# Handing the middle third of a bilinear sampler's sums to GpSimd, and turning each tile's samples one tile later

## What is computed

```python
x = x + _L0_conv_ref(_gn(x), ...)   # 8x8 patches, top-1 of 8 experts' 3x3 convolutions, ReLU
x = x + _L1_conv_ref(_gn(x), ...)   # 3x3 convolution whose weights are mixed from 4 by a routing
x = x + _L2_conv_ref(_gn(x), ...)   # nearest of 512 codebook vectors for every pixel
x = x + _L3_conv_ref(_gn(x), ...)   # bilinear sampling at 9 offsets per pixel, then a 3x3/stride-3 conv
```

## Time and profile before

| | before |
|---|---|
| median of 3 runs (lowest to highest) | 2382.57 us (2381.78 to 2383.68) |
| the profiled execution | 2377.75 us |
| its span | 2375.9 us |
| mean granted TensorE clock | 0.941 |
| busy PE / PE weight loads / DVE / ACT / POOL | 83% / 72% / 74% / 64% / 5% of the span |
| fronts | the instruction at L538, one in each front, starts from 233.8 to 2137.3 us |

### The profile page before, as it was taken

The page is one execution under the profiler, slowest core; times in us unless marked ns, Lnnn a source line. Parts: engine busy times, 40 slices in busy tenths (PEclk is TensorE's granted clock), DMA queues, the critical chain, the costliest instruction groups (busy, mean ns, idle before and its releaser), DMA issues.

```text
span 2375.9 us, 51549 instructions
## 1 busy us (share of the span) xinstructions
PE 1978.7 (83%) x20746; PEld 1699.7 (72%) x20746; DVE 1767.3 (74%) x3541; ACT 1525.7 (64%) x1787; POOL 111.6 (5%) x90
## 2 busy tenths in 40 slices
PE   0345579899798989989798898989799897989999
PEld 0212567789577976788677896778777895779998
DVE  2167368977698777987689876987679766997776
ACT  0022457677576865768576766767667675769886
POOL 2000000010000000010000100000000100001000
PEclk9877689999899998999899998999899998999999
DMA  6743854465444752556544763447535553223321
GB/s 185 147 118 94 188 143 140 134 170 160 119 138 127 192 163 89 174 120 173 140 144 124 186 168 106 163 112 191 153 113 159 143 147 98 71 74 114 115 108 52
DMA packets 258752, 323.93 MB, mean 136 GB/s; under 512 B 201268, under 2 KB 212244, under 8 KB 254292
## 3 DMA queue, kind: packets, MB, share of 16 engines
q1 hardware_dynamic: 240644, 274.52, 41.5%
q0 software_dynamic: 3280, 29.86, 5.1%
q10 hardware_dynamic: 14592, 16.26, 2.7%
HBM read 251.21 MB, written 55.99 MB: 129 GB/s over the span
## 4 chain that ended last, share of the span: by engine, by line
PE 47%; DVE 24%; DVEq 13%; issue 5%; DMA 4%; ACTq 3%; ACT 2%; SPq 2%; POOL 0%; POOLq 0%
PE bank L1105 33%; DVE samp L803 6%; DVEq L802 5%; DVE code L975 5%; DVEq L974 5%; PE bank L1092 3%; PE bank L1203 3%; PE bank L1162 3%; PE bank L1189 3%; DVE onehot L982 2%; SPq L392 2%; DVE top L973 2%; ACTq L588 1%; DVEq L999 1%; ACTq L638 1%
## 5 line engine op out<-in xcount | busy, mean ns | idle before, releaser
L1105 PEld LDWEIGHTS bank<-picture,tent 128*128 128x128 f32 x9216 | 1328.9, 195 | 145.2 <-issue 133.3
L1105 PE MATMUL bank<-picture,tent 128*128 128x160 f32 x9216 | 1391.1, 307 | 7.8 <-issue 4.5
L586 ACT ACTIVATE tent<-zs,row_at_sb 128x1152 f32<-128x1152 f32 x512 | 640.8, 1252 | 72.4 <-PE bank L1105 28.2
L798 DVE TENSOR_TENSOR strip<-bank,near 128x480 f32<-128x480 f32 x768 | 499.7, 651 | 215.7 <-PE bank L1105 214.2
L590 ACT ACTIVATE tent<-tent 128x2304 f32<-128x2304 f32 x256 | 543.9, 2125 | 18.8 <-issue 0.3
L803 DVE TENSOR_REDUCE samp<-strip 128x96 f32<-128x480 f32 x768 | 501.5, 653 | 70.9 <-issue 0.9
L1092 PE MATMUL bank<-ident_sb,samp 128*96 128x128 f32 x768 | 137.8, 290 | 179.9 <-DVE samp L803 118.7
L1203 PE MATMUL bank<-cb,xs 128*128 128x512 f32 x512 | 274.1, 618 | 14.1 <-ACT xs L654 7.9
L1092 PEld LDWEIGHTS bank<-ident_sb,samp 128*96 128x96 f32 x768 | 82.3, 130 | 206.8 <-DVE samp L803 145.0
L575 ACT COPY samp_t<-bank 96x384 f32<-96x384 f32 x256 | 119.7, 468 | 153.7 <-PE bank L1092 108.3
L654 ACT COPY xs<-xn 32x128 f32<-32x128 f32 x256 | 75.8, 296 | 171.6 <-PE bank L1203 154.8
(11 more groups left out here) (124 smaller groups left out, 1007.1 us busy)
## 6 DMA issues: line engine op xcount, KB each, us to landing
zs<-z_rows SPq DMA_DIRECT2D x256, 576.0 KB, 4.1
picked_weights<-arena SPq DMA_DIRECT2D x15, 1800.0 KB
arena<-picked_weights SPq DMA_DIRECT2D x24, 720.0 KB, 6.6
arena<-windows SPq DMA_DIRECT2D x288, 50.0 KB, 2.7
slice<-picked_weights SPq DMA_DIRECT2D x16, 720.0 KB, 6.7
windows<-arena SPq DMA_DIRECT2D x32, 312.5 KB, 6.1
slice<-windows SPq DMA_DIRECT2D x192, 50.0 KB, 2.3
arena<-xp SPq DMA_DIRECT2D x48, 136.0 KB, 4.9
```

The source lines that it names most:

```text
L586: act.activation(w[:, piece], zs[:, N % SPREADS, :], ACT.Abs, bias=row_at[:, piece:piece + 1])
L798: dve.tensor_tensor(y, STRIPS[J % 3][:, 0:DENSE * XW * C].rearrange("p (d c x) -> p d c x", d=DENSE, c=C), w.broadcast_to([128, DENSE, C, ...
L1105: m = pe.matmul(STRIPS[j % 3][:, XW * C * e:XW * C * (e + 1)], tent[:, N % TENTS, c, DENSE * d + e], picture[:, b % 2, i, c], start=(c == ...
```

## The change

- The middle third of each tile (`d == 1`) is multiplied by DVE but no longer summed by it: GpSimd adds its five columns in three instructions (192, 96 and 96 elements per partition), each waiting for the one before, and signals `middle_ready`. `strip` gets three buffers, one for each `d`; DVE's next middle multiply waits for `middle_ready`, and so does the turn. To make room in SBUF, `SPREADS` goes from 4 to 3.
- The turn of tile N-1 moves from behind the first third of tile N to behind its last third, `copy_samples` from `d == 1` one tile on to `d == 0` two tiles on, `convolve` from `d == 2` of tiles 4, 8, ... to `d == 1` of tiles 5, 9, ..., `copy_result` from `d == 0` to `d == 2` of these.
- `row1` and `row3` give a third each to `pool`, which has 5 now. They are spread over its steps: one between statistics and aggregation of the normalisation, one behind the normalisation, one before and one behind the routing product on DVE, one among the mixing instructions. ACT's exponent comes behind the second third of `pool` instead of behind all.
- GpSimd's own steps move: windows into `y`, the gathers behind `norm2` and behind half of `scores`, the subtraction behind the thirds of `rows`, the clip behind four thirds of `near`. SP's `store_weights(k, 1)` and `load_slice(k, 0)` come later.

```diff
-SPREADS = 4
+SPREADS = 3
-        strip = sb("strip", [128, 2, DENSE * C, XW])
+        strip = sb("strip", [128, THIRDS, DENSE * C, XW])
-        ... ("row0", 8), ("row1", 8), ("row2", 8), ("row3", 8), ("y", 7), ("features", 1), ("pool", 3),
+        ... ("row0", 8), ("row1", 7), ("row2", 8), ("row3", 7), ("y", 7), ("features", 1), ("pool", 5),
...
@@ SP, scores @@
-                    if t == 5 and k:
+                    if t == 6 and k:
                         store_weights(k, 1)
-                    if t == 6 and k:
-                        load_slice(k, 0)
                 at("spell")
                 at("pick")
+                if k:
+                    load_slice(k, 0)
@@ GpSimd @@
+            def third(J):
+                N, d = divmod(J, THIRDS)
+                if d != 1:
+                    return
+                y = strip[:, 1]
+                pool.wait_ge(strip_read, J + 1)
+                pool.tensor_tensor(y[:, :, 0:2], y[:, :, 0:2], y[:, :, 2:4], ALU.add).then_inc(summing, 1)
+                pool.wait_ge(summing, 2 * N + 1)
+                pool.tensor_tensor(y[:, :, 0], y[:, :, 0], y[:, :, 4], ALU.add).then_inc(summing, 1)
+                if N >= 2:
+                    pool.wait_ge(samp_turned, N - 1)
+                pool.wait_ge(summing, 2 * N + 2)
+                pool.tensor_tensor(samp[:, N % 2, PARTK:2 * PARTK], y[:, :, 0], y[:, :, 1], ALU.add
+                                   ).then_inc(middle_ready, 1)
@@ ScalarE @@
-                if d == 0 and N % SET == 1 and N > SET:
+                if d == 0 and N > 1:
+                    copy_samples(N - 2)
+                if d == THIRDS - 1 and N % SET == 1 and N > SET:
                     copy_result(N // SET - 1)
...
-                if d == 1 and N > 0:
-                    copy_samples(N - 1)
                 make_tent(N + 2, d)
...
-                at("pool")
+                at("pool", 0, 2)
                 act.wait_ge(z_ready, g + 1)
                 act.activation(sm1[:, 2], sm1[:, 1], ACT.Exp, scale=-1.0).then_inc(ez_ready, 1)
+                at("pool", 2)
@@ VectorE @@
+                if d == 1 and N > 0:
+                    dve.wait_ge(middle_ready, N)
...
+                if d == 1:
+                    return
                 if d == 0 and N >= 2:
                     dve.wait_ge(samp_turned, N - 1)
                 dve.drain()
-                m = dve.tensor_reduce(samp[:, N % 2, PARTK * d:PARTK * (d + 1)], strip[:, J % 2], AX.X, ALU.add)
+                m = dve.tensor_reduce(samp[:, N % 2, PARTK * d:PARTK * (d + 1)], strip[:, d], AX.X, ALU.add)
@@ TensorE @@
                 pe.wait_ge(samp_ready, N + 1)
+                pe.wait_ge(middle_ready, N + 1)
...
-                if d == 0 and N > 0:
+                if d == 1 and N % SET == 1 and N > SET:
+                    convolve(N // SET - 1)
+                if d == THIRDS - 1 and N > 0:
                     turn_samples(N - 1)
-                if d == THIRDS - 1 and N % SET == 0 and N > 0:
-                    convolve(N // SET - 1)
```

More of the change, by code:

```diff
@@ L267, in build @@
         reached = -SHIFT
-        for name, many in (("row0", 8), ("row1", 8), ("row2", 8), ("row3", 8), ("y", 7), ("features", 1), ("pool", 3),
+        for name, many in (("row0", 8), ("row1", 7), ("row2", 8), ("row3", 7), ("y", 7), ("features", 1), ("pool", 5),
                            ("mix", 3), ("conv1", 1), ("norm2", 3), ("scores", 4 * TILES), ("spell", 1), ("pick", 1),
@@ L547, in _, with at @@
             for g in range(GROUPS):
-                if g + 1 < GROUPS:
-                    windows(g + 1)
-                    for h in range(2):
-                        pick_weights(g + 1, h)
-                columns(g)
+                k = g + 1 if g + 1 < GROUPS else None
+                def at(name, first=0, end=None):
+                    for J in thirds_at(g, name, first, end):
+                        third(J)
+                for v in range(NV - 1):
+                    at(f"row{v}")
+                at("y", 0, 3)
+                if k:
+                    windows(k)
+                at("y", 3)
+                for name in ("features", "pool", "mix", "conv1", "norm2"):
+                    at(name)
+                if k:
+                    pick_weights(k, 0)
+                at("scores", 0, 4 * 4)
+                if k:
+                    pick_weights(k, 1)
+                at("scores", 4 * 4)
+                for name in ("spell", "pick", "norm3", "rows"):
+                    at(name)
+                subtract(g)
+                at("near", 0, 4)
+                clip(g)
+                at("near", 4)
+            for J in range(LEFT, THIRDS * ALL):
+                third(J)
         @engines.scalar
@@ L722, in _ @@
                 third(J)
+            copy_samples(ALL - 2)
             copy_samples(ALL - 1)
@@ L736, in norm @@
                 for h in range(2):
-                    if n < 2 or h > 0:
+                    if n == 0 or (n > 1 and h > 0):
                         stat(src, h)
@@ L919, in front @@
                     dve.wait_ge(conv1_done, 2 * g)
+                for h in range(2):
+                    stat(xres, h)
+                at("pool", 0, 1)
                 norm(g, 1, xres, grid1).then_inc(xn1_ready, 1)
-                at("pool", 0, 1)
+                at("pool", 1, 2)
                 dve.drain()
@@ L945, in front @@
                                                          op0=ALU.mult, op1=ALU.add)
+                    if e == 1:
+                        at("pool", 4)
                     dve.drain()
```

19 lines of the change are left out of this document (12 added, 7 removed).

## The result

The changed kernel takes 2315.07 us (median of 4 runs, 2312.38 to 2318.79); the kernel before, run beside it, 2382.18 us (4 runs, 2372.79 to 2383.68). The ratio is 0.9727, 95% interval 0.9698 to 0.9757: 2.7% faster, against 2320 us or 2.6% predicted. The profiled execution took 2312.38 us, its span 2310.6 us, its mean granted clock 0.944 (0.941 before).

A forecast was written before the change was run, and what follows sets the result against it. Bounds: VectorE and TensorE in scores, TensorE in the tail, neither from features to norm2. 7 x (-5.5 - 3) - 3.5 + 0.5 = -62.5 us gave 2315 profiled, 2320 median; range 2275 to 2372, the forecast's own 2280 to 2350.

The forecast's parts named there:

- Long stop: Features to norm2: TensorE's stop before pool's first turn, behind ScalarE's six DMAs, grows from 6.3 to some 10.5 us, +4.2.
- Second and third stop: Features to norm2: TensorE's second stop falls from 5.29 to about 2.2 us (-3.1); the third, 3.49, goes (-3.5).
- The clock: Features to norm2: TensorE's slowness after stops falls from 6 us to about 3, one long stop instead of three: -3.
- Scores: In scores, sums taken from VectorE gain 3 us a group (about 1 to 6.0); spacing of code_f near 11.9 us.
- The end and row0: Front's end gives 3.5 us; late zs with SPREADS = 3 takes it: 0 in six groups, -3.5 in the last.
- z: Front's end: VectorE's addition of z falls from 2.84 to about 0.46 us, the subtraction now standing behind the rows thirds.
- The tail: Tail: TensorE stays the limit, 0; the last tile's new order of sums and turns costs +0.5 at most.
- GpSimd's work: Each tile: three additions take 1.2 us with hand-overs, 2 as upper end, hidden before the next user.
- GpSimd against VectorE: Multiply with one PSUM input taken as free, 0.65 us; additions can hold single mixing, residual and perhaps comparison instructions.
- Slower: Rival, chance 0.11: GpSimd's additions hold VectorE's next multiply, +10.5 us a group in scores; +35.5 in all, about 2418 us.
- No or little gain: Rival, chance 0.13: long stop eats the exponent order's gain, late zs paid in full; 2358 to 2382, middle 2372 us.
- Larger: Rival, chance 0.10: front's end keeps its 3.5 us, long stop no longer than before; -130, about 2253 us.

The follow-up runs named there:

- e2: Changed kernel, with ScalarE copying the output that the first turn of pool waits for ahead of the root and its six DMAs: 2302.27 us.
- e10: Changed kernel with all sums on VectorE, two strip buffers and SPREADS = 4, so the new order alone (GpSimd's and SP's own steps at new places): 2316.60 us.
- e4: Changed kernel with the middle sums back on VectorE; order and buffers as after the change, GpSimd adds nothing: 2354.59 us.
- e11: e5 with the rows of one tile loaded between the second and third slice: 2342.26 us.
- e1: Changed kernel, with SP issuing the loads of one tile's rows between the second and third slice: 2275.51 us.
- e5: Kernel before with middle sums on GpSimd, third strip buffer, SPREADS = 3, GpSimd's and SP's own steps at new places; otherwise the old order: 2388.77 us.
- e9: Kernel before with SPREADS = 3 and nothing else: 2410.07 us.
- e8: Changed kernel with three more GpSimd additions of 192 elements in each tile, into columns nobody reads: 2339.50 us.
- e3: Changed kernel with the edits of e1 and e2 together: 2258.15 us.
- e12: e1 with two of ScalarE's pool thirds ahead of the root, exponent directly behind the DMAs, TensorE's routing product before pool's last third: 2211.61 us.
- e7: e3 plus samples copied ahead of the root, routing product before pool's last third, and the exponent directly behind the six DMAs: 2253.44 us.

## Why the prediction was right, and where it was not

The total (-62.5 against -65.4 between the two profiled executions) and the forecast's own range held, partly by luck: some terms were mis-sized, and their errors cancelled. Summed by groups: the first six of the seven were priced at -8.5 each, -51, and gave -49.1 (1630.4 to 1581.3 between the positions of the first and the seventh front); the last at -12, and gave -11.4 (273.0 to 261.6).

- **Long stop, its size and cause: right; its price is open.** 10.20 us for the 10.5, behind the six DMAs, so +3.9 for the +4.2 by length. (The +4.6 of the table is another quantity: a whole stage, with the 3.4 us of the two added thirds in it.) The prediction priced a stop by its length, and e2 shows that to be unsafe: there the stop was moved and 1.3 to 1.8 us a group were gained.
- **Second and third stop: right in kind.** The second shrank to 1.06 + 0.85, -3.4 for -3.1. The third has an heir that was not named, 2.63 us before the convolution for a copy of samples, so -0.9 for -3.5. The clock gave the 3 us: the slow records of the earlier trace rows cost 4.3 us, those of after about 1.2. From features to norm2 the sum is +4.6 - 5.7 - 3.4 = -4.5, with the 3.4 us of the two thirds that moved in, for the -5.5 taken.
- **Scores: -3.2 for -3, right as a sum, too small as the worth of the sums.** The order alone makes `scores` 1.2 us longer (107.7, e10), the sums make it 4.4 shorter. The steps of `scores` keep their length under the order; its extra lies ahead of the first of them (11.1 us for 10.1) and behind the last. Why was not tried. The sign that the prediction named, a step of 11.9 us, did not come: the earlier trace rows showed one of the short steps, and their mean (groups 2 to 6) went from 12.9 to 12.4. A further 2.3 a group is gained between conv1 and `scores` (19.8 to 17.5, e4), which the prediction did not give to the sums at all: it treated VectorE's time as worth something in `scores` only. Together the sums are worth 39.5 us, 5.6 a group, for 3: the largest term that was mis-sized, beside the late rows.
- **The end and row0: the wait was right, its price too small.** ScalarE stands 11.45 us for the 8.6 and TensorE 9.15, at the upper end of 6 to 9. The front's end gave 6.0 and not 3.5 (about 2.4 of it the sooner z, which the old order shows too in e11, and the rest the order), the late row took 6.9 and the rest of the rows gave 2.0: -1.1 for 0. The loss was priced at 4.6 (the 3.5 that it was to eat, and 1.1); e1 shows 6.6 a group, 39.6 in all. Both errors are over 2 us a group, and they nearly cancel.
- **z: right**, 0.46 us, in seven of eight fronts.
- **The tail: wrong.** Priced at +0.5, it gave -5.9. In e4 and e10, which have the order alone, it takes 233.5 us too; in e5, e9 and e11, which have the old order, 238.5 to 239.6. So it is the order, not the sums. Before, TensorE works 20.53 of the tail's first 23.3 us; after, 22.70 of 22.70 (the windows below). The earlier trace rows looked at 20 us in the middle, where TensorE is indeed never idle, and its two ends were not read. That is about half of it. The middle got shorter as well, though TensorE is busy all the time in both: from turn to turn a tile takes 5.29 us before (2332.82 to 2338.11) and 5.22 after (2271.42 to 2276.64), the turn behind three thirds itself 0.53 and 0.49. Why a turn takes longer there is not shown; a busy share of 100% hides it.

```profile
2136.70:2160.00 23.30, 20.53 (x167) 19.34 (x167) 19.21 (x27) 20.15 (x18) 7.79 (x2) 1.00 0.42 125
2160.00:2200.00 40.00, 40.00 (x331) 38.62 (x330) 28.46 (x44) 38.39 (x36) 0.00 (x0) 1.00 0.34 110
```

```profile
2077.30:2100.00 22.70, 22.70 (x189) 22.30 (x189) 16.70 (x27) 21.85 (x21) 13.28 (x14) 1.00 0.47 144
```

- **GpSimd's work: above the value taken, within its bounds.** 539 + 481 + 419 ns = 1.44 us a tile, 1.62 from the start of the first addition to the end of the last (the median), for 1.2 with hand-overs; hidden as said.
- **GpSimd against VectorE: right by the rows of before.** The multiply, which has one input in PSUM, is not held, and e8 confirms it: of the 768, 163 ran beside an addition of GpSimd, and these take 653 ns on average, none over 659. Of the others the prediction had only said that some could be held: the residual, with two inputs in SBUF, goes from 417 to 592 ns, the comparisons from 347 to 392. It is the additions that hold them. The 84 comparisons with one beside them take 486 ns, the other 172 take 347; and in e4 and e10, which have all but the additions, the residual takes 418 and the comparison 347. The Trainium skill (GPSIMD Engine Reference, section 8, Key points) says that GpSimd contends with VectorE instructions that have two SBUF inputs or run in a 2-port mode. The trace agrees: multiply 652 ns, residual 592. Four residuals in a row and the additions are shown below the list.
- **Rivals.** "Slower" is refuted by e8. "No or little gain" is what one gets from the sums with late rows in the old order (e5, 1.0038). "Larger" (about 2253 us) needed changes that the edit did not hold: with further edits e3 comes near it (2258.15) and e12 passes it.

The residual's four instructions of one front, before and after (VectorE), and the additions beside them (GpSimd, after):

```profile
1145.00 1.42 DVE L914 TENSOR_TENSOR kept<-kept,arena 128x256 f32<-128x256 f32 x4
```

```profile
1117.61 2.23 DVE L963 TENSOR_TENSOR kept<-kept,arena 128x256 f32<-128x256 f32 x4
```

```profile
1117.77 0.63 POOL L555 TENSOR_TENSOR strip<-strip 128x192 f32<-128x192 f32 x1 [3.70 <-DVE strip L845]
1118.48 0.53 POOL L557 TENSOR_TENSOR strip<-strip 128x96 f32<-128x96 f32 x1
1119.15 0.39 POOL L561 TENSOR_TENSOR samp<-strip 128x96 f32<-128x96 f32 x1
```

## What to carry to other kernels

What stands in an engine's queue behind a block of DMAs that it issues waits for the block (4.42 us for six on ScalarE here). Put the work that others wait for (a copy, a tent, one tile's loads) ahead of or into the block, and the block costs less. Here that was worth more (104 us from the change to e12, e1's 40 among them) than the offloaded sums (some 40). When a change bundles a reordering, an offload and a smaller buffer, measure each with the others held, and look for small moves that ride along: here the order with the early subtraction gave 63, the sums 41, and the smaller buffer took 40 back. In the old order nearly half of what the sums seemed to give is, by that estimate, the early subtraction's. A long wait is not its length in time: moving one copy ahead of the block took the 10.2 us stop away, left one of 7.7 us a turn later and gave 1.3 to 1.8 us a group; moving all that TensorE needs, with the routing product (e1 to e12), gave 9.1.

## What was not expected of the hardware

- GpSimd's small additions seem to have a large fixed part (an inference from these rows, which differ in their strides too): 96 elements a partition take 419 and 481 ns, 192 take 539 (536 in e8), while the earlier trace rows has 1440 elements in 2.73 us. Twice the elements add 0.06 to 0.12 us.
- In ScalarE's queue an exponent costs far more than its own 0.22 us, since a table load of 1.28 us comes with it: moved ahead of the tents it made the kernel 10.8 us slower (e7).
- The comparisons with 16-bit operands feel GpSimd's additions: 347 ns without, 392 with three and 436 with six of them a tile, while the multiply stays at 651 (e10), 652 and 652. Other work of GpSimd does not do it: in e10, 17 comparisons ran beside its gathers by indirect DMA, and took 348 ns.
